# Attention stage of a transformer layer: transposed blocks of neighbouring keys, weight splits two pairs ahead

## The reference

```python
latent_kv = x @ w_kv_down                 # x: 8 batches x 1024 tokens x 256
kv = latent_kv @ w_kv_up                  # rank 128 -> k and v, 16 heads of 64
q = (x @ w_q).reshape(Bx, Tx, 16, 64)
att = jnp.einsum('bqhd,bkhd->bhqk', q, k) * scale
att = jnp.where(causal, att, -jnp.inf)
att = jax.nn.softmax(att, axis=-1)
y = jnp.einsum('bhqk,bkhd->bqhd', att, v)
```

## Time and profile before

| | |
|---|---|
| Median of 3 runs | 3292.0 us (3286.45 to 3294.0) |
| The profiled execution | 3290.01 us, its span 3288.2 us |
| Busy in the span | PE 89%, DVE 70%, ACT 53%, POOL 48% |
| Mean granted TensorE clock | 0.951 of full speed |
| Attention stage | from 0 to about 2229 us |

### The profile page before, as it was taken

How to read it: one execution, slowest core, us unless ns; L and a number is a source line. 1 busy time by engine, 2 the same in 40 slices (tenths; PEclk the granted TensorE clock), 3 DMA queues, 4 the chain that set the end, 5 groups by cost and what they waited for, 6 DMA issues and landing times. The chain is left out here.

```text
span 3288.2 us, 53404 instructions
## 1 busy us (share of the span) xinstructions
PE 2916.1 (89%) x17196; PEld 1973.4 (60%) x17196; DVE 2307.4 (70%) x4808; ACT 1753.8 (53%) x3981; POOL 1568.3 (48%) x1661
## 2 busy tenths in 40 slices
PE   7898888888888898888888888869999999999997
PEld 4444444444444444444444444438999999999996
DVE  6777787776778777777687777863697875444546
ACT  5555555555555555555555555544544444444443
POOL 3334334344333433434433343424766777666665
PEclk9999999999999999999998999979999999999998
DMA  4666766676676666667667667677754444443435
GB/s 139 234 230 209 244 230 227 217 252 214 215 245 229 219 223 230 223 218 249 217 216 243 226 215 244 223 253 247 276 177 122 123 102 103 103 103 84 92 67 158
DMA packets 345525, 644.62 MB, mean 196 GB/s; under 512 B 36360, under 2 KB 244616, under 8 KB 337056
## 3 DMA queue, kind: packets, MB, share of 16 engines
q1 hardware_dynamic: 303200, 590.68, 53.0%
q0 software_dynamic: 25152, 33.75, 6.2%
q10 hardware_dynamic: 16896, 16.78, 1.5%
HBM read 347.38 MB, written 293.69 MB: 195 GB/s over the span
## 5 line engine op out<-in xcount | busy, mean ns | idle before, releaser
L214 POOL TENSOR_SCALAR prob<-prob,inv 128x256 f32<-128x256 f32 (+7 forms) x1024 | 748.6, 747 | 1286.4 <-DVE inv L667 1286.4
L524 ACT ACTIVATE prob<-s_ps,neg_max 128x128 f32<-128x128 f32 (+7 forms) x1024 | 755.6, 741 | 770.0 <-DVE neg_max L661 769.2
L661 DVE CUSTOM_DVE_ANT_0 s_ps<-s_ps,mask 128x128 f32<-128x128 f32 (+7 forms) x1024 | 754.7, 772 | 315.9 <-PE s_ps L340 315.6
L675 DVE STREAM_TRANSPOSE squares<-prob 128x640 f32<-128x640 f32 (+3 forms) x512 | 840.8, 1679 | 15.4 <-POOL prob L214 2.2
L386 PE MATMUL o_ps<-late_t,v 128*64 128x512 f32 (+3 forms) x2048 | 415.7, 528 | 22.7 <-DMA late_t<-s_d 20.8
L340 PE MATMUL s_ps<-tok 64*128 64x512 f32 (+3 forms) x1536 | 335.3, 542 | 55.0 <-ACT prob L524 54.1
L340 PE MATMUL s_ps<-k,q 64*128 64x512 f32 (+3 forms) x1536 | 328.3, 532 | 51.3 <-ACT prob L524 50.7
L1679 PE MATMUL e_y<-w_hi,hid_hi 128*128 128x256 f32 (+1 forms) x1088 | 312.1, 287 | 0.0
L1680 PE MATMUL e_y<-w_lo,hid_hi 128*128 128x256 f32 (+1 forms) x1088 | 308.0, 283 | 0.0
L1681 PE MATMUL e_y<-w_hi,hid_lo 128*128 128x256 f32 (+1 forms) x1088 | 308.0, 283 | 0.0
L1540 POOL DMA_INDIRECT acc_d<-yg,idx_all x128 | 211.0, 1649 | 189.7 <-ACT yg L1753 155.7
(11 more groups left out here) (233 smaller groups left out, 5594.1 us busy)
## 6 DMA issues: line engine op xcount, KB each, us to landing
s_d<-squares SPq DMA_DIRECT2D x64, 1024.0 KB, 5.4
late_t<-s_d SPq DMA_DIRECT2D x256, 256.0 KB, 4.3
s_d<-squares SPq DMA_DIRECT2D x64, 896.0 KB, 4.0
late_t<-s_d SPq DMA_DIRECT2D x256, 224.0 KB, 5.2
s_d<-squares SPq DMA_DIRECT2D x64, 768.0 KB, 3.6
late_t<-s_d SPq DMA_DIRECT2D x256, 192.0 KB, 4.5
s_d<-squares SPq DMA_DIRECT2D x64, 640.0 KB, 2.9
late_t<-s_d SPq DMA_DIRECT2D x256, 160.0 KB, 4.3
```

The costliest lines, as they stand in the source:

```text
L214: pool.tensor_scalar(pr, pr, inv[:, i:i + 1], 1.0, ALU.mult, ALU.mult).then_inc(norm_done, 1)
L524: act.activation(prob[i][:, 0:(q + 1) * P], score_part(n, s), ACT.Exp, scale=-1.0, bias=neg_max[:, i:i + 1], accum_out=total[:, i:i + 1]). ...
L661: dve.tensor_tensor_reduce(part, part, mask[:, T - (q + 1) * P:T], 1.0, -MASKED, ALU.add, ALU.min, neg_max[:, i:i + 1]).then_inc(max_done, 1)
L675: dve.transpose(square_all(q).rearrange("p (j h k c) -> p j h k c", j=4, h=2, c=Q)[:, :, h, :, :], prob[(2 * q + h) % PB][:, 0:t * P].rear ...
```

## The change

There are three edits. The transpose's source is read so that square j holds the 32 neighbouring keys 32j + c. The DMA of j then fills the 32 neighbouring partitions 32j to 32j+31. And the weights of pair n+2, in place of n+1, are rounded by ACT at the start of slot 5 of pair n and split by POOL at the end of slot 4; those of pairs 0 and 1 are done ahead of the loop.

```diff
@@ POOL
-            weights_low(0)
+            for n in range(2):
+                weights_low(n)
...
-                if q == 1 and n + 1 < NPAIRS:
-                    weights_low(n + 1)
+                if q == 4 and n + 2 < NPAIRS:
+                    weights_low(n + 2)
@@ SP, read_squares
-                    sp.dma_start(late_t[n % 2][j:P:4, q - 4, :, 0:2 * t * Q],
+                    sp.dma_start(late_t[n % 2][Q * j:Q * j + Q, q - 4, :, 0:2 * t * Q],
@@ ACT
-            weights_high(0)
+            for n in range(2):
+                weights_high(n)
...
                 if q == 1:
                     exp(n, 2)
-                    if after:
-                        weights_high(n + 1)
                     exp(n, 3)
...
                 if q == 5:
                     if after:
                         keep(n + 1, 3)
+                    if n + 2 < NPAIRS:
+                        weights_high(n + 2)
                     exp(n, 10)
                     exp(n, 11)
@@ DVE, turn_squares
-                                  prob[(2 * q + h) % PB][:, 0:t * P].rearrange("p (k c j) -> p j k c", j=4, c=Q)
+                                  prob[(2 * q + h) % PB][:, 0:t * P].rearrange("p (k j c) -> p j k c", j=4, c=Q)
```

## The result

The changed kernel took 3603.7 us (median of 3 runs) against 3292.0 us: 1.0957 times the time before, interval 1.0922 to 1.0992. Its span in the profile is 3599.5 us, 311 us more than before. The direction was forecast, the size was not: 3380 us, and a range up to 3510. One of e8's four executions, which took 4853 us at a granted clock of 0.716, is left out of its ratio.

The account below looks back on a forecast made before the run. PE, the busiest engine, was followed through its waits. An ordinary pair of 32.95 + 1.5 (clock) + 1.4 (reads) = 35.85 us adds 123 us over 54 pairs: 3290.0 + 123 - 35 = 3378, given as 3380; range 3210 to 3510.

Parts of the forecast that it names:

- The transposes: DVE ahead of exp 7: unstepped transposes at 1211 and 1079 ns, S4 2.8 us earlier, 0.80 us of later waits removed.
- PE's wait for `w_lo`: Ahead of `project_q`: not worth its 2.47 us, since PE would stand at S4 till 1012.14 just the same.
- The weights' place: ACT's rounding ahead of exp 10 waits for the load; S6 starts 1.04 us after exp 10, at 1023.1.
- The load's landing: Last weight load of SP's turn lands at 1021.5 in place of 1023.42, before any cost of slower reads.
- half of 2.9 us for the reads: Reads into 32 neighbouring partitions, ahead of the weights in the queue: between 0 and 2.9 us, 1.4 taken.
- The move up of SP's turn: SP's issue of the load moves up by 1.46 + about 0.45 = 1.9 us.
- the reads at the full price: Rival: the reads cost 2.9 us, a pair takes 37.35 us, 3460 us in all; chance 18%.
- The clock: From S6 on, PE's slow clock after 3.6 us idle: bounds 0 and 2.07 us, 1.5 taken.
- Pairs that end a batch: Longer slots 3 and 4 let the load land in time; these pairs keep 3.6 us: -25 us.
- The last terms of the sum: Outside the 54 pairs: -25 for batch ends, -7 for pairs 62 and 63, -3 for last transposes; -35 us.
- the mean of 33.58 us: Average ordinary pair before the change, from 29 pairs; the forecast pair of 35.85 us was 2.27 more.

Follow-up runs that it names:

- e8: Kernel before, with neighbouring keys per square, reads still to every fourth partition, ACT's slot 0 to 3 exps and latent product reordered to match: 3107.7 us, 0.9448.
- e5: Kernel before, with the weights moved as in the change and SP issuing their load ahead of the write of q = 7: 3350.4 us, 1.0195.
- e6: The changed kernel, with the weights of pair n+2 rounded at the start of ACT's slot 7 and split behind POOL's norm of slot 6: 3344.8 us, 1.0176.
- e12: The changed kernel, with SP issuing the weights' load ahead of the write of q = 7: 3346.0 us, 1.0193.
- e3: Kernel before, with only the transposes' source changed (keys in another order than v's): 3095.8 us, 0.9424.
- e1: The changed kernel without the weights' move, so transposes and DMA destination only: 3304.3 us, 1.0054 of the kernel before.
- e4: Kernel before, with only the reads' destination changed to 32 neighbouring partitions (keys in another order than v's): 3383.0 us, 1.0301.

## Why the prediction was wrong in size

- **The transposes: right.** They take 1224 and 1089 ns against 1211 and 1079 taken. S4 comes 2.86 us sooner against 2.8, S7 to S1 is 0.59 us shorter, and PE's wait for `w_lo` is not worth its 2.5 us (e5): all as worked out. That the maximum, another instruction, took so nearly the same time was luck: no row showed a transpose without a step.
- **The weights' place: right in mechanism and place.** ACT waits for wv in slot 5, exp 10 behind it, PE at S6. S6 follows the landing by about 1.5 us, 1.6 taken. e6 and e12 take ACT's wait away in two ways, and each gives some 258 us back.
- **The load's landing: the step that failed.** "The load lands at 1023.42 - 1.9 = 1021.5", and half of 2.9 us for the reads, put it 23.2 us behind S1; it landed at 26.3, 3.1 us later. Two terms were mis-sized. The move up of SP's turn was 1.9 us in the text and 1.35 in e3 (24.0 to 22.6). And "I take half, 1.4 us" for the reads, with an upper end of 2.9, was 3.7 us (e3 to e1, 22.6 to 26.3; about as much from the kernel before to e4), more than the upper end. The last 0.3 us are the pair that was read, whose load landed sooner than the average pair's. The bound of 2.9 came from halving the best rate, 436 GB/s; but the stretch ran at 192 GB/s, under that half. The weights' own DMAs add little: the load lands 0.6 us behind the last read (1.1 before), so its 7.3 us are mostly waiting behind the reads. The Trainium skill (SBUF — State Buffer, the section on the DMA port swizzle) gives 189 GB/s for a transfer of 1 MiB to partitions 0 to 31, and the trace agrees, with 192 in its full stretch (here reads of 224 and 256 KB queued one behind another). The rival "the reads at the full price" was nearer with 3460 us, and still 140 us short: it shared the other misses, and its 2.9 us for the reads were too little as well.
- **The clock: right in mechanism, 0.5 us too small.** 1.5 us were taken, between the bounds 0 and 2.07; S6 to S7 grew by 1.76, and by 2.05 if the wait of 0.29 that went away is counted.
- **Pairs that end a batch: wrong.** "The load lands in time" there: it did not. In them S1 to S5 took 4.8 us less than before, but S5 to S6 took 7.37 us in place of 3.85, and S6 to S7 1.8 us more. They cost what they had cost before (39.2 us against 39.3) instead of 25 us less in all, although without ACT's wait they gain even more than forecast: they take 33.5 us in e1. The last terms of the sum, -35 us, came to about -4.

Of the 224 us between 3380 and 3604, (39.30 - 35.85) x 54 = 186 are the ordinary pairs: the landing 3.1 x 54 = 167 and the clock 0.5 x 54 = 27, less 8 because S6 followed the landing a little sooner. About 31 are the pairs and ends that were to gain. Another 6 are the mean of 33.58 us, which was read from 29 pairs and is 0.11 above that of all 54.

## What to carry to other kernels

Before work that depends on a DMA is moved ahead, find that DMA's landing in the trace and set it beside the new place: here it landed behind it already before the change. A layout that speeds up one engine must be priced on the DMA queue too, and if both ends of that price are unknown, a run of each half of the change by itself is worth more than the middle between them. A wait that looks removable can be what hides something else (here a slow stretch of TensorE's clock), so after removing it look at what follows the place where the waiting went.

## What the runs showed of the hardware

- A VectorE transpose of float32 that reads its source with a step of four elements took 2010 ns for 1024 columns, and 1224 with a step of one.
- ScalarE's exp from PSUM, writing float32 to SBUF with a step of four elements (its reads without a step), took 1180 ns for 512 columns, and 682 with a step of one.
- A read from DRAM into 32 partitions was slow where these lay in one half of 64 (steps of one and two) and fast where they lay over all 128 (step of four): 23% more time of the queue's packets over the whole kernel, 18% with a step of two. Issuing the reads by turns into one half and the other gave back a quarter of it.
- Ten matmuls without use in each ordinary pair, in a place where TensorE had idled 3.3 us, raised the mean granted clock from 0.950 to 0.982 and saved 83 us.
